# A decoder kernel on one NeuronCore: the scan's result is turned by VectorE blocks and DMAs, and two passes over h are put behind the chain of x

## The reference, cut to what matters

```
x = layernorm(x + attention(x))            # 16 heads of 32, LoRA merged into the weights
state[t] = decay[head] * state[t-1] + ctx[t] * ctx[t]
x = layernorm(x + x * state)               # "cross attention" is this scan
h = layernorm(gelu(silu(bitlinear(x, w1, b1)))) * ln_g + ln_b
x = layernorm(x + bitlinear(h, w2, b2))    # bitlinear: rms norm, rows to 8 bit, ternary weights
```

## Time and profile before

| | |
|---|---|
| runs | 1050.31, 1051.01, 1052.35 us |
| profiled execution | 1050.39 us, its span 1048.6 us |
| mean granted clock of TensorE | 0.962 |
| PE busy | 950.2 us (91%) |
| DVE busy | 891.9 us (85%) |
| ACT busy | 827.4 us (79%) |
| POOL busy | 605.4 us (58%) |
| chain that ended last | PE 60%, DVE 26%, DMA 6%, ACT 4% |
| DMA to landing | z transposes 3.2 us, x transposes 3.4 us, ctx 3.8 us (medians) |

### The profile page before, as it was taken

How to read it: one execution, slowest core, us unless ns; L and a number is a source line. 1 busy time by engine, 2 the same in 40 slices (tenths; PEclk the granted TensorE clock), 3 DMA queues, 4 the chain that set the end, 5 groups by cost and what they waited for, 6 DMA issues and landing times.

```text
span 1048.6 us, 23525 instructions
## 1 busy us (share of the span) xinstructions
PE 950.2 (91%) x9388; PEld 655.1 (62%) x9388; DVE 891.9 (85%) x1474; ACT 827.4 (79%) x957; POOL 605.4 (58%) x767
## 2 busy tenths in 40 slices
PE   5998997999999999999999999999999999978416
PEld 3766756676767767676767767676767677644102
DVE  4577868989898999989898989899898989995766
ACT  3646686888979797988888797978889797977684
POOL 2332337474766749485757658494757566572653
PEclk9999998999999999999999999999999999988668
DMA  9432200213122121323131121323231321122213
GB/s 357 158 111 113 72 3 21 74 52 84 23 71 61 43 76 52 84 52 83 35 100 23 56 68 44 83 52 84 52 84 21 79 56 54 42 52 63 53 30 91
DMA packets 106352, 73.68 MB, mean 70 GB/s; under 512 B 91386, under 2 KB 91386, under 8 KB 104451
## 3 DMA queue, kind: packets, MB, share of 16 engines
q1 hardware_dynamic: 105522, 70.34, 24.2%
q10 hardware_dynamic: 720, 1.84, 0.5%
HBM read 41.73 MB, written 8.40 MB: 48 GB/s over the span
## 4 chain that ended last, share of the span: by engine, by line
PE 60%; DVE 26%; DMA 6%; ACT 4%; issue 3%; POOL 1%; SPq 0%; POOLq 0%; DVEq 0%; ACTq 0%
PE bank L1333 21%; PE bank L1467 11%; PE bank L1474 9%; DMA xqT<-xq 5%; PE wave L1382 4%; PE bank L1396 4%; PE wave L1358 3%; DVE neg_max L962 3%; DVE h L1085 3%; PE bank L1400 3%; DVE stats L1013 3%; PE bank L1468 3%; DVE fz L1090 2%; DVE rows L1029 2%; DVE qx L1052 1%
## 5 line engine op out<-in xcount | busy, mean ns | idle before, releaser
L962 DVE TENSOR_REDUCE neg_max<-wave 128x8 f32<-128x2048 f32 x64 | 146.2, 2284 | 39.0 <-PE wave L1358 39.0
L547 POOL TENSOR_TENSOR h<-h,g_tile 128x2048 f32<-128x2048 f32 x30 | 139.9, 4663 | 39.1 <-ACT h L738 39.1
L655 ACT ACTIVATE probs<-wave 128x1024 f32<-128x1024 f32 x128 | 124.4, 1024 | 40.5 <-PE wave L1382 40.3
L1467 PE MATMUL bank<-w,xqT 128*128 128x512 fp8e4 x496 | 129.7, 384 | 20.6 <-DMA xqT<-xq 20.6
L437 POOL TENSOR_SCALAR attn_hi<-attn 128x256 fp32r<-128x256 f32 x64 | 31.8, 497 | 150.1 <-DVE attn L995 134.8
L717 ACT ACTIVATE h<-bank,qx 128x512 f32<-128x512 f32 x124 | 83.8, 689 | 24.4 <-PE bank L1468 22.1
L693 ACT ACTIVATE rows<-rows,rstd 128x512 f32<-128x512 f32 x96 | 74.3, 807 | 33.1 <-POOL rstd L453 18.5
L1085 DVE TENSOR_TENSOR h<-h,b_tile 128x2048 f32<-128x2048 f32 x32 | 84.0, 2624 | 17.0 <-POOL h L547 16.9
L1467 PEld LDWEIGHTS bank<-w,xqT 128*128 128x128 bf16 x496 | 47.8, 99 | 78.0 <-issue 17.4
L1474 PE MATMUL bank<-w,hqT 128*128 128x512 fp8e4 x416 | 94.3, 380 | 0.0
L496 POOL TENSOR_TENSOR rows<-rows,bo_tile 128x512 f32<-128x512 f32 x32 | 52.6, 1665 | 71.2 <-DMA rows<-x 71.2
(11 more groups left out here) (181 smaller groups left out, 2844.1 us busy)
## 6 DMA issues: line engine op xcount, KB each, us to landing
ctx_sb<-ctxT SPq DMA_DIRECT2D x16, 512.0 KB, 3.8
rows<-x SPq DMA_DIRECT2D x16, 512.0 KB, 4.0
out<-rows SPq DMA_DIRECT2D x32, 256.0 KB, 2.5
xT_in<-xT SPq DMA_DIRECT2D x15, 512.0 KB, 4.7
h<-w1T SPq DMA_DIRECT2D x4, 1024.0 KB, 14.6
h<-w2T SPq DMA_DIRECT2D x4, 1024.0 KB, 4.8
h<-Wq SPq DMA_DIRECT2D x1, 1024.0 KB, 6.2
h<-Wk SPq DMA_DIRECT2D x1, 1024.0 KB, 9.8
```

The source lines that it names most:

```text
L547: po.tensor_tensor(h_of(b, q)[:, :], h_of(b, q)[:, :], g_tile[:, :], ALU.mult).then_inc(done, 1)
L655: ac.activation(probs[:, kt, :, :], wave[:, :, kt * T:(kt + 1) * T], ACT.Exp, scale=SM_SCALE).then_inc(S["probs_ready"], 1)
L962: dv.tensor_reduce(neg_max[:, :, :], wave[:, :, :].rearrange("p j (t k) -> p j t k", t=NT), axis=AX_X, op=ALU.max, negate=True).then_inc(S ...
L1467: pe.matmul(p[:, :], xqT[:, q, kc, :], w1[:, kc, n * FW:(n + 1) * FW], start=(kc == 0), stop=False)
```

## The change

The scan's result is no longer turned by PE. At the end of `scan`, two DVE transposes turn each 32x32 block of it in place of position, out of `ctx_sb` into `x_round` (free at that time), 512 elements on each partition and instruction. At the start of the next body SP issues `move_state`: 16 DMAs, for each pair of a source and a destination group of 32 partitions, that put the blocks where a full transpose has them, back into `ctx_sb`. Each moves 32 x 8 runs of 128 bytes. `layernorm2_sum` waits for them and reads SBUF in place of PSUM, and the load of the next ctx waits for these sums. PE's eight transposes and their two bank uses go.

Four passes change their place. POOL's second `g_mul` goes behind `inverse_std2` and `x_rms`. DVE's second `z_add` goes behind `quantise_x`. ACT's first `z_square` goes behind both `normalise(2)`, its second behind `ctx_square`. In the drain, f(6) and f(7) of the last batch wait for the last probs where they waited for `ln2`.

```
+SB = P // HD
...
-            (DV, "scan_done", 5), (DV, "ln1", 6), (DV, "ln2", 6), (DV, "x_quant", 14),
+            (DV, "scan_done", 7), (DV, "ln1", 6), (DV, "ln2", 6), (DV, "x_quant", 14),
...
+            (SP, "state_moved", 16 * SB * SB),
...
-                 ("r", 0, 1, "ln2", 1), ("r", 1, 1, "ln2", 4), ("v", 0, -1, "v_stored", 1),
-                 ("v", 1, -1, "v_stored", 2)]
+                 ("v", 0, -1, "v_stored", 1), ("v", 1, -1, "v_stored", 2)]
...
+        state_blocks = flat(x_round[:, :, :])
+        state_rows = flat(ctx_sb[:, :, :])
...
             def load_ctx(b):
-                wait(sp, "rT_ready", b - 1, 2)
+                wait(sp, "ln2", b - 1, 4)
...
+            def move_state(b):
+
+                wait(sp, "scan_done", b, 7)
+                for a in range(SB):
+                    for s in range(SB):
+                        to = state_rows[s * HD:(s + 1) * HD, :].rearrange("p (n a c) -> p n a c", a=SB, c=HD)
+                        block = state_blocks[a * HD:(a + 1) * HD, s * T:(s + 1) * T]
+                        sp.dma_start(to[:, :, a, :],
+                                     block.rearrange("p (n c) -> p n c", c=HD)).then_inc(S["state_moved"], 16)
...
             def body(j):                                   # SP
                 if alive(j, -1):
                     load_xT(j + 1)
+                move_state(j - 1)
                 if alive(j, 3):
                     transpose_z(j - 3, 1)
...
             def drain():
+                move_state(LAST)
                 transpose_z(THIRD, 1)
...
                     attn_split(j, 1)                       # POOL
-                if alive(j, 2):
-                    g_mul(j - 2, 1)
                 if alive(j, 1):
                     inverse_std2(j - 1)
                     x_rms(j - 1)
+                if alive(j, 2):
+                    g_mul(j - 2, 1)
                 if alive(j, 3):
                     inverse_std3(j - 3, 1)
...
-                if alive(j, 2):                            # ACT
-                    z_square(j - 2, 0)
                 if alive(j, 1):
                     normalise(2, j - 1, 0)
                     normalise(2, j - 1, 1)
+                if alive(j, 2):
+                    z_square(j - 2, 0)
...
                     probs_of(j, 3)
-                if alive(j, 2):
-                    z_square(j - 2, 1)
...
                     ctx_square(j)
                 if alive(j, 2):
+                    z_square(j - 2, 1)
                     zq_store(j - 2, 0)
...
                                  ALU.max).then_inc(S["scan_done"], 1)      # DVE, end of scan
+                wait(dv, "scan_done", b, KC + 1)
+                wait(dv, "xq_stored", b - 1, 1)
+                blocks = state_blocks.rearrange("p (s q k c) -> p q k s c", s=SB, q=NT, c=HD)
+                for q in range(NT):
+                    dv.transpose(blocks[:, q, :, :, :],
+                                 ctx_sb[:, :, q * P:(q + 1) * P].rearrange("p k (s c) -> p k s c", c=HD)
+                                 ).then_inc(S["scan_done"], 1)
...
-                wait(dv, "rT_ready", b, q + 1)
+                wait(dv, "state_moved", b, 16 * SB * SB)
                 wait(dv, "norm1", b, q + 1)
-                dv.scalar_tensor_tensor(rows_of(b)[:, q, :], bank_of("r", q, b), SCAN_SCALE, rows_of(b)[:, q, :],
-                                        ALU.add, ALU.mult).then_inc(S["ln2"], 1)
+                dv.scalar_tensor_tensor(rows_of(b)[:, q, :], state_rows[:, q * D:(q + 1) * D], SCAN_SCALE,
+                                        rows_of(b)[:, q, :], ALU.add, ALU.mult).then_inc(S["ln2"], 1)
...
-                if alive(j, 2):                            # DVE
-                    z_add(j - 2, 1)
                 if alive(j, 1):
                     quantise_x(j - 1)
                 if alive(j, 2):
+                    z_add(j - 2, 1)
                     quantise_z(j - 2, 0)
...
-                wait(pe, "scan_done", LAST, 5)             # PE, drain
-                for q in range(NT):
-                    r_product(bank_of("r", q, LAST), q)
...
-                drain_f(6, "ln2", LAST, 1)
-                drain_f(7, "ln2", LAST, 4)
+                drain_f(6, "probs_ready", LAST, 8)
+                drain_f(7, "probs_ready", LAST, 8)
...
                     shiftT(j, 2)                           # PE, body
-                if alive(j, 1):
-                    r(j, 0)
-                    if j == 1:
-                        pe.wait_ge(u_scale, 5)
-                    r(j, 1)
-
-                if alive(j, 0):
                     shifted(j, 2)
```

More of the change, by code:

```diff
@@ L160, in decoder_kernel @@
             (PE, "shifted_ready", 4), (PE, "scores_ready", 4), (PE, "qk_ready", 4), (PE, "v_ready", 2),
-            (PE, "shiftT_ready", 4), (PE, "pv_ready", 4), (PE, "o_ready", 2), (PE, "rT_ready", 2),
+            (PE, "shiftT_ready", 4), (PE, "pv_ready", 4), (PE, "o_ready", 2),
             (PE, "f_ready", 8), (PE, "y_ready", 2),
@@ L205, in half_rows, with flat @@
             return t.rearrange("p (i k) -> p i k", i=2)[:, :, 0:INNER // 2]
+        def flat(t):
+            return t.rearrange("p a b -> p (a b)")
         def rows_of(b):
@@ L217, in decoder_kernel @@
         LAST, PRIOR, THIRD = NB - 1, NB - 2, NB - 3
-        drain_bank = {("o", LAST, 0): 7, ("o", LAST, 1): 6, ("r", LAST, 0): 2, ("r", LAST, 1): 3,
+        drain_bank = {("o", LAST, 0): 7, ("o", LAST, 1): 6,
                       ("y", THIRD, 0): 0, ("y", THIRD, 1): 1, ("y", PRIOR, 0): 4, ("y", PRIOR, 1): 5,
@@ L254, in ffw @@
             return h[FFW_BUFFER[n]][:, :]
-        def flat(t):
-            return t.rearrange("p a b -> p (a b)")
         def merge_bank(m, kc):
@@ L1447, in o_second_half @@
                 split_product(bank_of("o", q, j - 1)[:, :], o_terms(q, (2, 3)), first=False).then_inc(S["o_ready"], 1)
-            def r(j, q):
-                r_product(take(j, "r", q, "scan_done", j - 1, 5), q)
-            def r_product(p, q):
-                for kc in range(KC):
-                    last = pe.transpose(p[:, kc * P:(kc + 1) * P], ctx_sb[:, kc, q * P:(q + 1) * P], ident[:, :])
-                last.then_inc(S["rT_ready"], 1)
             def f(j, u):
@@ L1643, in body @@
                     shifted(j, 3)
+                if j == 1:
+                    pe.wait_ge(u_scale, 5)
                 if alive(j, -1):
```

## The result

The changed kernel took 1144.8 us, the median of four runs (1137.46 to 1149.74), beside 1050.66 for the kernel before on the same chip: 1.0888 times as long, 95% interval 1.0824 to 1.0952. The prediction, 1113 with a range of 1090 to 1134, had the side right and the size wrong: 32 us of the loss stood outside it. The profiled execution took 1149.74 us, its span 1147.9; it is the slowest of the four, 4.9 us above the median.

A forecast was written before the change was run, and what follows sets the result against it. PE was taken to bound the kernel, busy 57.25 of 58.00 us a body. Twelve periods of +5.1 us with the end effects gave +62.3 on a span of 1048.6, so 1113 us in all, range 1090 to 1134.

The forecast's parts named there:

- PE's transposes: Eight PE transposes removed from a body: 1.4 us with their wait, of which about 0.38 us would be gained.
- rival A: At DVE's shift instruction L969 (later L984): g_mul does not delay it, the kernel is faster, 1042 us; chance 0.15.
- DVE's block transposes: Two at the end of scan, 1.5 us with the semaphore wait; mostly hidden, rest costed at nothing, 0.4 us without cover.
- SP's 16 DMAs: Issues ahead of y(j, 1)'s DMA transposes, 0.43 to 0.59 us each, 6.9 to 9.4 together; nothing, upper bound 1 us.
- Rival C: SP's issues at 0.8 us each end 4.1 us late, 3 us past the spare: 36 us more, 1149; chance 0.08.
- The load of ctx: It waits for the second layer norm's second sum, some 2 us later, with over 10 us until ctx_square; nothing.
- The sums from SBUF: Second layer norm's sums on DVE: 0.68 us from PSUM, taken as equal from SBUF, bounds -0.1 and +0.3 us each.
- the hold-up: DVE's L969 (later L984), with two SBUF inputs, waits for POOL's running g_mul: 4.25 us on DVE in each body.
- ACT's z_square: Both passes come later on ACT, the first still ending before PE needs the shift copy; nothing, at most 0.5 us.
- g_mul behind x_rms: POOL's g_mul, moved later, is running when DVE's L969 arrives and delays it; with PE's slower clock 5.1 us a body.
- B: DVE's L969 is delayed by g_mul but PE's clock does not slow: 3.9 us a body, 1099 us; chance 0.20.
- The sum: Twelve periods x 5.1 = +61.2, body 15 +3, drain -0.9, body 1 gains about 1: +62.3, giving 1113 us.

The follow-up runs named there:

- d4: Kernel before with PE turning only one block in four (2 transposes a body instead of 8): 1052.0 us, ratio 0.9995.
- a2: Changed kernel with only 4 of SP's 16 DMAs, g_mul still late: 1114.1 us, ratio 1.0569.
- b1: Kernel before with only the moves in instruction order (g_mul, z_add, z_square later), PE still turning the scan result: 1108.6 us, ratio 1.0521.
- b4: Changed kernel with g_mul waiting until behind the shift, and SP's 16 DMAs divided, 10 ahead of hqT's DMA transposes, 6 behind: 1074.6 us, ratio 1.0220.
- d1: Kernel before with the moves in order and g_mul waiting until behind the shift, PE still turning the scan result: 1068.9 us, ratio 1.0139.
- d5: b4 with DVE's two block transposes cut to one block each (128 x 32) for every batch but the first: 1068.9 us, ratio 1.0145.
- after: The changed kernel itself, with the whole change against the kernel before: 1144.8 us, ratio 1.0888.
- a1: Changed kernel with g_mul put back ahead of inverse_std2 and x_rms, all 16 DMAs kept: 1120.8 us, ratio 1.0634.
- a3: Changed kernel with g_mul put back early and only 4 of the 16 DMAs: 1109.1 us, ratio 1.0524.
- d3: Kernel before with the second layer norm's sum reading a constant SBUF tile in place of PE's PSUM bank, g_mul early: 1106.7 us, ratio 1.0504.
- b2: Kernel before with z_add behind quantise_x and both z_square later, g_mul early, PE still turning the scan result: 1053.2 us, ratio 1.0010.
- c1: Changed kernel with each of the 16 DMAs moving 32 runs of 1 KB in place of 256 of 128 bytes: 1140.4 us, ratio 1.0824.
- a4: Changed kernel with g_mul waiting until behind the shift, SP's 16 DMAs undivided: 1097.4 us, ratio 1.0462.

## Why the prediction was wrong

**PE's transposes.** Priced at a gain of 0.38 us a body, which went into rival A and not into the 5.1. d4 shows 0.04 for six of the eight: the chain of x through DVE sets the body, and a faster PE waits for it. The estimate had looked only at the next instruction on PE.

**DVE's block transposes.** The duration was right, 1.30 us for two against 1.5 with the wait. "I cost the rest at nothing" was not: the turn with four DMAs costs 0.34 us a body (a2 against b1), 0.5% of the time; the prediction had 0.4 as its bound. With the gate and the divided issues the turn costs 0.8% (b4 against d1), and cutting it short gives 0.7% back (d5 against b4).

**SP's 16 DMAs. This is the step that failed.** "I take nothing, upper bound 1 us". An issue takes 0.61 us, next to the 0.59 of the earlier trace rows, but there are 0.04 us between two, and in every body from 3 to 15 one of the sixteen takes 1.0 to 2.0 us (in body 8 the seventh, 1.75): 11.56 us against 9.4 at most, and 10.8 to 12.0 over these bodies. They start at 541.34, 1.4 us behind the clamp as forecast, and end 12.9 us behind it, against 10.2 of the old issue time. PE waited 2.69 us in that body and then ran at a clock of 0.66: the transposes went out 2.8 us later and the second landed 1.3 us slower than the median, so the spare was 1.4 us, close to the "about 1" of the prediction. Over the 13 bodies the waits are 1.88 us in the mean, and five slow `y(j, 1)` of 1.69 us more add 0.65: 2.53, next to the 2.42 us a body (3.2%) that separate a2 and after. That is the price with `g_mul` late; with `g_mul` early it was 0.24. Rival C described this mechanism, with its place and its threshold of 0.6 us, but it was given 0.08. That its 1149 is within 5 us of the result is in part luck: it has 36 us for the queue, the periods show 29, and the ends make up for it. Its price for an issue was near too: 0.72 in the mean (11.56 / 16) for 0.8.

**The load of ctx** cost nothing: PE's list has no wait for it.

**The sums from SBUF**, "taken as equal": right in the kernel after (0.68 us), but only because `g_mul` stood elsewhere. The prediction named them as candidates for the hold-up and dropped them, as POOL has only a short instruction there now. It didn't ask the question that a1, a3 and d3 answer: with this operand `g_mul` can't stay where it was, either.

**ACT's z_square**, "nothing, at most 0.5 us": b2 has PE waiting 1.0 us for the copy of the shift behind it, which takes the place of the wait for xqT. As forecast, xqT is in time (no wait in bodies 3 to 14), and as b2 shows that is worth nothing.

**g_mul behind x_rms.** Right at every step: both chains start at the last statistics, `g_mul` starts 0.54 us ahead of L984 (forecast 0.4), L984 takes 4.01 us in 13 bodies (4.25 to 4.4), PE waits 4.2, or 3.4 in b1 (4.0), and the clock falls (0.68 and 0.62 over the next 4.2 and 4.5 us). 4.67 us a body in b1 against 5.1, 12 x 4.67 = 56 of the 61 us forecast. Rival A (no hold-up) and B (no slower clock) are excluded by these rows.

**The sum.** 12 x 5.1 = 61.2 became 12 x 7.43 = 89.2: 4.67 for the order, 0.34 for the turn, 2.42 for the queue. Outside the 12 periods the profiled execution is 10.1 us longer, for a forecast of 1: 5.8 ahead of the third layer norm's sum of body 3 (235.75 against 229.99), 4.4 behind that of body 15. Of the signs that the prediction named, the hold-up, `g_mul`'s start and the missing wait for xqT came; the window of a body is 65.53 us and not 62 to 63.5, and SP's issues end at 552.90, behind ACT's `zq_store(j-3, 1)` (550.25). What stays open is how the long issue among the sixteen and the slow landings of hqT come about, and how the 16 us of the gated order in d1 divide between its short holds, the longer scans, the waits for `silu` and the later `z_square`.

No version here beats the kernel before. The best that makes the whole turn on DVE and SP, b4, is 2.2% slower (1.9 to 2.5), and b2 and d4 show that neither the z passes nor six of PE's eight transposes had anything to give that can be measured.

## What to carry to other kernels

When a VectorE operand moves from PSUM to SBUF, look at what GpSimd runs beside it: here one operand cost 5%, in a kernel with nothing else changed, and moving the GpSimd pass only moved the loss to another instruction with two SBUF inputs. A DMA that replaces work on a compute engine costs its issue on the queue and whatever stands behind it: multiply the count by the issue time and the gaps, add something for a long one (1 to 2 us in each series of after), and compare the end with the due time of the next entry, since dividing the sixteen around it gave back 23 us. Price the thing removed by the wait that comes next on the critical chain: six of PE's eight transposes were worth 0.04 us a body. And look at more than one body before a duration is made a reason: the scans' time in body 8 of b4 and d5 said the opposite of the whole traces.

## What the runs showed of the hardware

* A VectorE instruction on 128x8 or even 128x2 values is held until the end of a running GpSimd pass when both of its inputs are in SBUF: 4.01 us for 0.17 behind `g_mul` in after, 1.27 for 0.16 in b4. With one input in PSUM the same pass cost it nothing (0.68 us for 512 columns beside `g_mul`, in the kernel before), and one operand moved to SBUF made it 4.20 (d3).
* A scan of 128x256, with `decay_col` and `ctx_sb` in SBUF, takes 0.67 us alone and about 1.7 beside a GpSimd sum: 2.43 us for four with none held, 4.53, 5.58 and 6.65 with two, three and four held.
* The hold works both ways: `g_mul` took 5.11 us for 4.65 where a sum was running when it came (d3).
* A DMA issue on SP takes 0.61 us for 256 runs of 128 bytes and 0.59 for 32 runs of 1 KB (medians), with 0.04 us between two and one of 1.0 to 2.0 us in each series of after. Sixteen take 11.56 and 10.70 us in body 8 of after and c1, with the DMA engines 26% and 17% busy.
* PE's clock after a wait is not told by the wait's length alone: in after `y(j, 1)` took 5.30 us for 3.61 behind waits of 1.99 us and more, in a4 it took 3.61 behind all 13, up to 2.70 us.
